# Layer 1's expert rows: stored at the tokens' places inside the expert loop, or gathered from the slots' places in the last sum

## The reference, cut to what matters

```python
h = _layernorm(x, axis=-1) * (1 + cb) + sb
x = x + gb * _L1_ffn_ref(h, ...)          # the last operation: x is the output

def _L1_ffn_ref(x, gate_w, gate_b, expert_bias, w1, b1, w2, b2):
    gate_logits = jnp.einsum('bsd,ed->bse', x, gate_w) + gate_b + expert_bias
    top_idx = jnp.argmax(gate_logits, axis=-1)
    out = jnp.zeros_like(x)
    for e in range(NUM_EXPERTS):
        mask = (top_idx == e)[..., None].astype(x.dtype)
        h = jax.nn.relu(jnp.einsum('bsd,df->bsf', x, w1[e]) + b1[e])
        y = jnp.einsum('bsf,fd->bsd', h, w2[e]) + b2[e]
        out = out + mask * y
    return out
```

## Time and profile before

| | us |
|---|---|
| median of 3 runs | 1347.14 |
| lowest, highest | 1346.67, 1350.69 |
| the profiled execution | 1345.81 |
| its span in the profile | 1343.9 |
| busy in the span: PE, DVE, POOL, ACT | 959.7, 983.7, 684.5, 544.3 |
| layer 1's expert loop, first gather to last matmul | 1211.3 to 1293.8 |
| the last sum, first gather to the end of the span | 1297.5 to 1343.9 |

### The profile page before, as it was taken

How to read it: one execution, slowest core, us unless ns; L and a number is a source line. 1 busy time by engine, 2 the same in 40 slices (tenths; PEclk the granted TensorE clock), 3 DMA queues, 4 the chain that set the end, 5 groups by cost and what they waited for, 6 DMA issues and landing times. The chain is left out here.

```text
span 1343.9 us, 15247 instructions
## 1 busy us (share of the span) xinstructions
PE 959.7 (71%) x4580; PEld 620.7 (46%) x4580; DVE 983.7 (73%) x2121; ACT 544.3 (41%) x1128; POOL 684.5 (51%) x436
## 2 busy tenths in 40 slices
PE   3858776977797686656859963689697987458950
PEld 3423223422342141125859961356465666358950
DVE  6449899899979999986967744666676666664522
ACT  2244653464356444321024431344546464305630
POOL 0066485657555856614057737746325335207726
PEclk9968888988898988985579985989798989758975
DMA  6034233333333333422013332101000000042313
GB/s 165 0 129 151 103 149 133 126 129 144 138 125 129 139 143 125 157 94 63 1 40 97 97 62 52 33 6 27 1 1 1 17 1 17 17 157 60 75 51 100
DMA packets 53217, 109.31 MB, mean 81 GB/s; under 512 B 8913, under 2 KB 38801, under 8 KB 44817
## 3 DMA queue, kind: packets, MB, share of 16 engines
q1 hardware_dynamic: 46480, 94.70, 20.2%
q0 software_dynamic: 6656, 13.64, 4.5%
HBM read 94.17 MB, written 14.16 MB: 81 GB/s over the span
## 5 line engine op out<-in xcount | busy, mean ns | idle before, releaser
L661 POOL TENSOR_TENSOR ma_bu<-ma_u,ma_bc 128x1024 f32<-128x1024 f32 x128 | 299.6, 2359 | 173.3 <-DMA ma_bc<-bc_rows 118.1
L700 DVE TENSOR_TENSOR_SCAN decay_ps<-decay_ps,ma_bu 128x512 f32<-128x512 f32 x256 | 320.6, 1252 | 30.8 <-ACT decay_ps L592 22.8
L498 PE MATMUL y_ps<-ma_h,ident 128*128 128x512 f32 x512 | 270.0, 646 | 78.1 <-DVE ma_h L710 78.1
L592 ACT ACTIVATE decay_ps<-ma_delta,negA 128x512 f32<-128x512 f32 x256 | 175.7, 690 | 226.4 <-DVE ma_h L710 225.7
L498 PEld LDWEIGHTS y_ps<-ma_h,ident 128*128 128x128 f32 x512 | 92.5, 199 | 250.6 <-DVE ma_h L710 181.1
L956 POOL DMA_INDIRECT s_rows<-xs,take x112 | 124.5, 1111 | 125.0 <-POOLq L776 88.6
L710 DVE TENSOR_TENSOR ma_h<-decay_ps,ma_bc 128x512 f32<-128x512 f32 x256 | 172.4, 674 | 0.0
L973 PE MATMUL s_up_ps<-s_xt,s_w 128*128 128x128 f32 x896 | 122.6, 281 | 0.0
L973 PEld LDWEIGHTS s_up_ps<-s_xt,s_w 128*128 128x128 f32 x896 | 113.3, 198 | 0.0
L982 PE MATMUL s_out_ps<-s_w,s_ht 128*128 128x128 f32 x608 | 86.1, 276 | 0.7 <-DVE s_outs L1049 0.7
L1225 POOL DMA_INDIRECT mi_y<-ys,where x64 | 63.5, 992 | 36.3 <-POOLq L932 18.3
(11 more groups left out here) (256 smaller groups left out, 1777.6 us busy)
## 6 DMA issues: line engine op xcount, KB each, us to landing
ma_bc<-bc_rows SPq DMA_DIRECT2D x64, 1024.0 KB, 4.6
ys<-s_outs SPq DMA_DIRECT2D x28, 256.0 KB, 2.5
w<-in_experts SPq DMA_DIRECT2D x1, 4112.0 KB, 13.4
xs<-rows SPq DMA_DIRECT2D x8, 512.0 KB, 3.2
w<-in_experts SPq DMA_DIRECT2D x1, 3072.0 KB, 10.1
out<-X SPq DMA_DIRECT2D x8, 256.0 KB, 2.3
s_rows<-xs,take POOLq DMA_INDIRECT x112, 2.8
su_cw<-in_L_conv_row SPq DMA_DIRECT2D x2, 512.0 KB, 5.3
```

What stands on the lines that cost most here:

```text
L498: mm = pe.matmul(y_ps[j][:, col(c)], m.ident[:], h[g % HS][:, col(c)], start=False, stop=True, skip_group_check=True)
L592: act.activation(decay[s % DS][:], delta[b % 2][j][:, col(c)], ACT.Exp, scale=m.negA0[:, j, n:n + 1]).then_inc(decay_done, 1)
L661: pool.tensor_tensor(bu[g % BUS][:], u[b % 2][j][:], bc[q % BCS][:, 0, :], ALU.mult).then_inc(bu_done, 1)
L700: dve.tensor_tensor_scan(dst, d[:], bu[g % BUS][:, col(c)], past if c else 0.0, ALU.mult, ALU.add).then_inc(scan_done, 1)
```

## The change

Layer 1's expert loop no longer stores slots in their own order. For each slot, POOL issues an indirect store that writes the 128 rows of `outs` to the places of their tokens in `m.ys[1]`. It stands LAG = 13 places behind in POOL's order: store s comes behind gather s+13 and waits for the read-out of slot s. The read-out of a group's first slot now waits for the four stores of the group two back. SP stores nothing in layer 1's loop. In `combine` the rows are in the tokens' order, so four plain loads of 512 KB bring them (SP issues two, ACT two), each into a buffer of its own, and POOL has no part in it.

Empty rows of a slot need a place to go. The tables `m.xs` get one more row, NOBODY = 2048, filled with zeros in `setup` (tokens from 2048 on lie one row further). `m.take` now points there for an empty row, by an add of NOBODY in place of the cast on L910. A new table `m.put` holds the place where each row is stored, equal to `m.take` for a token's row, and a row of its own behind the tokens' (from the table `aside`, one more load in `setup`) for an empty one. Two more DVE operations in layer 1's `route` compute it.

```diff
@@ setup, SP
             load(m.ids[:], a["ids"])
+            load(m.aside[:], a["aside"])
...
+            for layer in range(2):
+                load(m.xs[layer][NOBODY:NOBODY + 1, :], a["nobody"], big, n_big)
             sp.wait_ge(big, 16 * n_big[0])
@@ route, DVE
             dve.wait_ge(taken, 1)
-            then(dve.tensor_copy(m.take[:, 0:slots], take_ps[:]))
+            then(dve.tensor_scalar(m.take[:, 0:slots], take_ps[:], float(NOBODY), None, ALU.add))
+            if layer == 1:
+                then(dve.scalar_tensor_tensor(beside[:], take_ps[:], 0.0, m.aside[:], ALU.is_equal, ALU.mult))
+                then(dve.scalar_tensor_tensor(m.put[:], beside[:], float(NOBODY), take_ps[:], ALU.add, ALU.add))
@@ sorted_experts
+    LAG = 13
+    STORES = (1, GROUP)
...
-            pool.wait_ge(m.rows_stored, 16 * NBATCH * (layer + 1))
-            for s in range(slots):
+            def gather(s):
                 if s >= ROWS:
                     pool.wait_ge(turned, base + s - ROWS + 1)
                 pool.indirect_dma_start(rows[s % ROWS][:], None, m.xs[layer], bass.IndirectOffsetOnAxis(
                     ap=m.take[:, s:s + 1], axis=0)).then_inc(fetched[s % ROWS], 16)
+
+            def scatter(s):
+                g = s // GROUP
+                pool.wait_ge(out_read, base + s + 1)
+                pool.indirect_dma_start(m.ys[1], bass.IndirectOffsetOnAxis(ap=m.put[:, s:s + 1], axis=0),
+                                        outs[g % 2][:, s % GROUP, :], None).then_inc(stored[g % 2], 16)
+
+            pool.wait_ge(m.rows_stored, 16 * NBATCH * (layer + 1))
+            for i in range(slots + (LAG if layer == 1 else 0)):
+                if i < slots:
+                    gather(i)
+                if layer == 1 and i >= LAG:
+                    scatter(i - LAG)
...
                 if t == 0 and g >= 2:
-                    dve.wait_ge(stored[g % 2], 16 * (base // (2 * GROUP) + g // 2))
+                    dve.wait_ge(stored[g % 2], 16 * STORES[layer] * (g // 2))
...
@@ combine
-        @block.gpsimd
-        def _(pool):
-            for g in range(GROUPS):
-                if g >= BUFFERS:
-                    pool.wait_ge(x_done, g - BUFFERS + 1)
-                for t in range(g * GROUP, (g + 1) * GROUP):
-                    pool.indirect_dma_start(y[g % BUFFERS][:, t % GROUP, :], None, m.ys[1], bass.IndirectOffsetOnAxis(
-                        ap=m.where[:, 0, t:t + 1], axis=0)).then_inc(fetched[g % BUFFERS], 16)
+        def load(engine, b):
+            first = row_of(b * SEQ)
+            engine.dma_start(y[b][:], m.ys[1][first:first + SEQ, :].rearrange("(t p) d -> p t d", p=P)
+                             ).then_inc(fetched[b], 16)
+
+        @block.scalar
+        def _(act):
+            for b in range(1, NBATCH, 2):
+                load(act, b)
...
         @block.sync
         def _(sp):
+            for b in range(0, NBATCH, 2):
+                load(sp, b)
             for g in range(GROUPS):
                 sp.wait_ge(x_done, g + 1)
```

More of the change, by code:

```diff
@@ L22 @@
 EPS = 1e-5
+NOBODY = TOKENS // 2
 D_IN = 256
@@ L42, with row_of @@
     pass
+def row_of(token):
+    return token + (token >= NOBODY)
 SORTED_SEMS = ("copied turned turn_read up_done act_done ht_done out_done out_read fetched0 fetched1 fetched2 "
-               "fetched3 fetched4 fetched5 fetched6 fetched7 stored0 stored1")
+               "fetched3 fetched4 fetched5 fetched6 fetched7 stored0 stored1 scattered0 scattered1")
 def setup(nc, a, m):
@@ L790, in route @@
         owner = sb("owner", [1, slots])
+        beside = sb("beside", [P, slots])
         take_ps = ctx.enter_context(nc.psum_tensor(tag + "take_ps", [P, slots], F32))
@@ L946, in sorted_experts @@
         fetched = [sem(f"fetched{i}") for i in range(ROWS)]
-        stored = [sem(f"stored{i}") for i in range(2)]
+        stored = [sem(f"stored{i}" if layer == 0 else f"scattered{i}") for i in range(2)]
         block = ctx.enter_context(nc.Block())
@@ L1066, in _ @@
         def _(sp):
[L1067 to L1070, removed]
+            if layer == 0:
+                for g in range(slots // GROUP):
+                    sp.wait_ge(out_read, base + (g + 1) * GROUP)
+                    sp.dma_start(m.ys[0][g * GROUP * P:(g + 1) * GROUP * P, :].rearrange("(q p) d -> p q d", p=P),
+                                 outs[g % 2][:]).then_inc(stored[g % 2], 16)
             for r in range(2):
-                sp.wait_ge(stored[r], 16 * ((base + slots) // (2 * GROUP)))
+                sp.wait_ge(stored[r], 16 * STORES[layer] * (slots // (2 * GROUP)))
 def combine(nc, m):
@@ L1082, in combine @@
         sem = lambda name: m.kept.enter_context(nc.semaphore("c1_" + name))
-        y = [sb(f"y{i}", [P, GROUP, P]) for i in range(BUFFERS)]
-        fetched = [sem(f"fetched{i}") for i in range(BUFFERS)]
+        y = [sb(f"y{b}", [P, BT, P]) for b in range(NBATCH)]
+        fetched = [sem(f"fetched{b}") for b in range(NBATCH)]
         gated, x_done, stored = sem("gated"), sem("x_done"), sem("stored")
         block = ctx.enter_context(nc.Block())
-        @block.gpsimd
-        def _(pool):
-            for g in range(GROUPS):
-                if g >= BUFFERS:
-                    pool.wait_ge(x_done, g - BUFFERS + 1)
-                for t in range(g * GROUP, (g + 1) * GROUP):
-                    pool.indirect_dma_start(y[g % BUFFERS][:, t % GROUP, :], None, m.ys[1], bass.IndirectOffsetOnAxis(
-                        ap=m.where[:, 0, t:t + 1], axis=0)).then_inc(fetched[g % BUFFERS], 16)
+        def load(engine, b):
[6 more added lines that the diff above has]
+                load(act, b)
         @block.vector
@@ L1778, in build @@
         m.take = sb("take", [P, max(SLOTS)], mybir.dt.uint32)
+        m.put = sb("put", [P, SLOTS[1]], mybir.dt.uint32)
+        m.aside = sb("aside", [P, SLOTS[1]])
         m.weight = sb("weight", [P, 2, TILES])
@@ L1801, in build @@
         m.gb1 = sb("gb1", [P, 2, NE])
-        m.xs = [nc.dram_tensor(f"xs{layer}", (TOKENS, P), F32).ap() for layer in range(2)]
-        m.ys = [nc.dram_tensor(f"ys{layer}", (SLOTS[layer] * P, P), F32).ap() for layer in range(2)]
+        m.xs = [nc.dram_tensor(f"xs{layer}", (TOKENS + 1, P), F32).ap() for layer in range(2)]
+        m.ys = [nc.dram_tensor("ys0", (SLOTS[0] * P, P), F32).ap(), nc.dram_tensor("ys1", (TOKENS + 1 + SLOTS[1] * P, P), F32).ap()]
         m.out = out
@@ L1888 @@
     arrays["ident"] = np.eye(P, dtype=np.float32)
+    arrays["aside"] = (TOKENS + 1 - NOBODY + np.arange(SLOTS[1] * P, dtype=np.float32)).reshape(SLOTS[1], P).T.copy()
+    arrays["nobody"] = np.zeros((1, P), np.float32)
     arrays["identb"] = np.eye(P).astype(mybir.dt.np(BF16))
@@ L1893 @@
     arrays["count"] = np.arange(P, dtype=np.float32)
-    arrays["ids"] = np.arange(TOKENS, dtype=np.float32).reshape(TILES, P).T.copy()
+    arrays["ids"] = np.array([row_of(token) - NOBODY for token in range(TOKENS)], np.float32).reshape(TILES, P).T.copy()
     nc = bacc.Bacc("TRN2", target_bir_lowering=False, num_devices=1)
```

14 lines of the change are left out of this document (6 added, 8 removed).

## The result

The changed kernel takes 1353.53 us (median of 11 runs, 1350.26 to 1356.7), the kernel before 1348.53 us (11 runs, 1344.07 to 1350.89). The ratio is 1.0037 [1.0024, 1.005]: slower by about 5 us, where 2.4 us faster was forecast. 1353.5 lies in the range that was given, but 8.8 us above the value.

What follows compares the result with a forecast made beforehand. Layer 1's loop was taken as TensorE-bound, then 46 us behind it paced by POOL's gathers; POOL would bound the new loop. Span 1324.0 + 3.2 + 11.6 + 2.7 = 1341.5, -2.4 us; forecast 1344.7, range 1337 to 1355.

Steps and rivals of the forecast that it cites:

- Last landing to next block: Behind layer 1's loop: POOL's 0.9 us start behind the old store's landing taken over, from 1323.1 to 1324.0.
- First load: In the sum: first 512 KB load lands after 3.2 us, from a possible 3.2 to about 6.
- The loop: Layer 1: bound moves from PE to POOL; 79 steps of 1.25 us, 98.8, plus 10 us for 40 weight copies.
- rival 1: Layer 1's loop: an indirect store costs POOL more than a gather; at 1.10 us slower by about 4 us; chance 0.17.
- rival 2: Layer 1's loop: copies fall in step with POOL, 0.48 us a copy, 9.2 us more, 1353.9; chance 0.10.
- rival 3: Layer 1's loop: copies cost POOL only 0.08 to 0.12 us each, 5 to 7 us less, 1338.7; chance 0.13.
- VectorE's wait for landed stores: Layer 1's loop: read-outs wait for stores two groups back; PE stands still some 3.4 us per group, off the path.
- Rival 4: Layer 1's loop: PE's stalls lower its granted clock to 1.2 GHz, up to 7 us more, 1351.7; chance 0.04.
- The first gather: Start of layer 1's loop: 0.5 us later than 1211.27, from two more DVE operations in `route`.
- VectorE's pairs: In the sum: DVE's 8 pairs of operations take 8 x 1.45 = 11.6 us.
- the landing: End of layer 1's loop: the last indirect store lands 2.5 us after its start; ends 2.4 and 3.5.

Runs made afterwards that it cites:

- e1: Changed kernel with the last sum in the same block as layer 1's expert loop: 1380.55 us, ratio 1.0028 to the kernel before, second sort of chips.
- e8: Changed kernel with layer 1's weight copies on ScalarE and ReLU on VectorE, sum in the loop's block, `aside` loaded late: 1338.97 us, 0.9934 to the kernel before.
- e9: Changed kernel with the sum in the loop's block and all four of its loads issued by SyncE: 1383.4 us, ratio 1.0031 to the kernel before.
- e10: Changed kernel without 33 of 40 weight copies in layer 1's loop, computation incomplete: 1345.32 us, ratio 0.9977 to the kernel before.

## Why the prediction was wrong

**The step that failed** is "Last landing to next block: ... POOL started 0.9 us behind: 1324.0". It measured 5.5 us. The 0.9 us came from a place at which GpSimd had been idle for 22.6 us (the idle time stands in the row of 1297.49); whatever it needs to close a block was long over. The change moves GpSimd's last work to the end of the block, and I asked only when the data had landed, not when the engine was through. Of the 7.4 us between the forecast difference and the measured one (-2.4 and +5.0), 4.6 are this, and e1, e8 and e9 show it.

The trace of before had rows that tell it. At the end of the middle, where GpSimd's last operation (2.35 us) starts at 1176.31, VectorE and SyncE wait for a block's end:

```profile
1176.31 2.35 POOL L1236 TENSOR_TENSOR rows<-rows,shift_row 128x1024 f32<-128x1024 f32 x1
...
1178.68 0.36 SPq L1215 DMA_DIRECT2D xs<-rows  x1
1184.19 0.61 SPq L916 DMA_DIRECT2D w<-in_experts  x1
1184.25 0.43 DVE L845 TENSOR_TENSOR r_lg<-logits,gb 128x256 f32<-128x256 f32 x1 [5.73 <-PEq L1156]
```
```profile
SPq L1156 <- PEq L1156: 4.9, 1, 4.9
```

5.5 us from the end of GpSimd's last operation (1178.66) to the next block, on the path. Counted so from the end of the last store's issue, 1321.5 + 5.5 = 1327.0 stands where the sum had 1324.0, and the forecast would have been 0.6 us more than before instead of 2.4 less. In the trace of after, the same stretch, from the end of the last issue to the first load, is 6.8 us.

**First load, 3.2 us**: measured 4.8 (4.7 to its landing). This was the term that I took from the low end, although I had written that four loads are under way together; the Trainium skill's sentence that was weighed there ("DMA: Bandwidth & Descriptors", Issuing engines are not separate DMA queues), that transfers of all issuing engines interleave on the same DMA engines, has no figure; the 5 to 6 us that I estimated by it were nearer. e9 shows 0.9 us of it as sharing with ScalarE's loads.

**The loop, 108.8 us**: right in mechanism and nearly in size, 110.6 and 108.9. The bound moved to GpSimd, the store costs it little more than a gather (0.983 against 0.944 and not 1.10, so rival 1 is out, with 40 x 0.04 = 1.6 us), and a copy costs 0.20 to 0.25 us, as taken; rival 2 (0.48) and rival 3 (0.08 to 0.12; the stretches it leaned on had 0.12 and 0.15, so its lower end had no row) are out. The two small errors, store and copies, partly cancelled: some luck in a term that came out near.

**VectorE's wait for landed stores**: foreseen as a stall off the path. It is larger than I made it (39.0 us in 7 pieces), and off the path, as e10 shows. Rival 4: TensorE's granted clock was 0.88 on average between 1234 and 1308, after the gaps had begun, and GpSimd still waited for nothing. (The 47 matmuls in 5 us of that rival are not in the earlier trace rows, which give 541 in 60, or 45; the price hardly changes.)

**The first gather, +3.3 us**: `route` took the 0.5 us foreseen (VectorE's three operations at 1213.30, 1213.53 and 1213.77). The rest is for the most part the quick execution that the sum was made against. It doesn't enter the difference of medians: the kernel before's median in the result, 1348.53, is 2.7 us above that execution. By differences: -2.4 forecast; +1.8 loop, +4.6 block, +1.6 load, -0.9 pairs, -0.2 landing give +4.5, and 5.0 was measured.

**VectorE's pairs** took 1.33 us and not 1.45; the landing 2.3 us as against 2.5.

## What to carry to other kernels

When a change makes an engine the last to work in a block, price its end of the block from a place where it really came last, not from one where it had been idle. Where loads need only the data, let them wait for the stores' semaphore in the same block: 5 to 7 us here. Where GpSimd issued DMAs without a pause, every microsecond that VectorE copied in SBUF cost it 0.26 to 0.40 us. Such copies are worth trying on ScalarE if it has room, even if it is slower at them: 7 us here on the first sort of chips, nothing that shows on the second. So a gain that lives on GpSimd's issue rate has to be measured on more than one chip.

## What was not expected of the hardware

GpSimd's end of a block came 2.9 to 7.0 us behind its last operation: 5.3 behind plain arithmetic in the middle, 4.8 and 2.9 behind gathers (layer 1's loop and the sum of before), 6.6 and 7.0 behind layer 0's gathers (before and after), 6.6 behind the stores, by the traces' single records. What sets the length is open. An indirect store into DRAM cost GpSimd 0.965 to 0.999 us and landed in 2.3 us, as a gather does. And the two sorts of measurement differ by 2% in this kernel: of the 24.1 us between the two traces of before, 17 lie in layer 0's expert loop and 5.5 in layer 1's, stretches in which GpSimd issues indirect DMAs without a pause, in whole or in part, and other engines start up to several us late.
